# Partial sums of a graph kernel dealt out anew over its first half, and placed between two groups of count products

## Time and profile before

| | |
|---|---|
| median of three runs | 971.59 us |
| the profiled execution | 978.19 us, of which the span is 976.4 us |
| TensorE (matmul) busy | 858.0 us, 88% of the span |
| VectorE, ScalarE, GpSimd busy | 637.5, 418.0, 648.1 us |
| mean granted clock of TensorE | 0.85 of full |
| first gather to last gather | 47.3 to 722 us |
| first gate products of the second half | 765.2 us |

### The profile page before, as it was taken

One profiled execution on the slowest core, in us unless ns is written; L12 is line 12 of the kernel. 1 busy time (PEld: TensorE's weight loads), 2 busy tenths in 40 slices (PEclk: granted clock), 3 DMA queues, 4 the chain that ended last, 5 costly groups with the idle time before them and its releaser, 6 DMA issues.

```text
span 976.4 us, 15073 instructions
## 1 busy us (share of the span) xinstructions
PE 858.0 (88%) x5101; PEld 690.2 (71%) x5101; DVE 637.5 (65%) x1329; ACT 418.0 (43%) x811; POOL 648.1 (66%) x975
## 2 busy tenths in 40 slices
PE   5955797769988988999999998999988999999795
PEld 5845585556767887877788876888875666666473
DVE  5353677676776759677976785777754354556853
ACT  5522345543554546454665544555522221111241
POOL 4598988888888888888888888888860011111000
PEclk9955658785676669678999997999968999999998
DMA  9355133444444444454555554455542465555210
GB/s 201 71 124 161 55 68 96 129 124 123 99 135 99 111 116 128 130 127 121 142 153 155 147 143 111 117 150 153 139 109 64 123 189 147 156 160 177 74 37 21
DMA packets 59396, 119.20 MB, mean 122 GB/s; under 512 B 16593, under 2 KB 36751, under 8 KB 56189
## 3 DMA queue, kind: packets, MB, share of 16 engines
q1 hardware_dynamic: 39810, 93.29, 30.2%
q0 software_dynamic: 18448, 24.82, 15.7%
q10 hardware_dynamic: 1056, 0.07, 0.1%
HBM read 81.34 MB, written 36.68 MB: 121 GB/s over the span
## 4 chain that ended last, share of the span: by engine, by line
POOL 49%; PE 32%; issue 7%; DVE 7%; DMA 3%; SPq 1%; ACT 1%; DVEq 0%; ACTq 0%; POOLq 0%
POOL shared L836 25%; POOL cnt_rows L841 13%; POOL zs_third L836 11%; PE bank L2285 7%; PE bank L2315 4%; PE bank L2117 4%; PE bank L2284 3%; PE bank L2170 3%; PE bank L2037 2%; PE bank L2316 2%; DVE zus L1113 2%; DMA shared<-zu_table,src_col 1%; PE bank L2202 1%; PE bank L1940 1%; PE bank L2220 1%
## 5 line engine op out<-in xcount | busy, mean ns | idle before, releaser
L836 POOL DMA_INDIRECT shared<-zu_table,src_col x306 | 297.4, 972 | 52.1 <-issue 49.2
L841 POOL MEMSET cnt_rows<- 54x300 f32 x450 | 165.2, 367 | 0.3
L836 POOL DMA_INDIRECT zs_third<-zu_table,src_col x144 | 140.9, 978 | 23.2 <-issue 23.2
L2037 PEld LDWEIGHTS bank<-zus,shared 125*128 125x128 f32 x900 | 139.1, 247 | 16.8 <-issue 13.1
L2037 PE MATMUL bank<-zus,shared 125*128 125x64 f32 x900 | 141.4, 333 | 7.4 <-ACT setup L1803 3.0
L2170 PE MATMUL bank<-layer,oh 128*125 128x84 f32 x900 | 136.0, 325 | 0.8 <-DVE layer L1199 0.8
L2170 PEld LDWEIGHTS bank<-layer,oh 128*125 128x125 f32 x900 | 133.3, 240 | 1.1 <-issue 1.1
L1113 DVE TENSOR_TENSOR setup<-iota_b,bank 128x500 bf16<-128x500 bf16 (+1 forms) x224 | 124.5, 609 | 8.0 <-PE bank L2242 7.8
L1746 ACT ACTIVATE shared<-shared,node_id 125x2304 f32<-125x2304 int32 x25 | 55.4, 2216 | 97.5 <-PE bank L2037 59.0
L859 POOL DMA_DIRECT2D shared<-counts_table x22 | 11.7, 535 | 101.9 <-PE bank L2285 90.9
L1803 ACT ACTIVATE setup<-bank 125x500 bf16<-125x500 f32 (+1 forms) x91 | 57.3, 680 | 49.7 <-PE bank L2242 48.4
(11 more groups left out here) (254 smaller groups left out, 1700.4 us busy)
## 6 DMA issues: line engine op xcount, KB each, us to landing
shared<-in_edges SPq DMA_DIRECT2D x25, 1125.0 KB
own_table<-own_out SPq DMA_DIRECT2D x25, 375.0 KB
counts_table<-setup SPq DMA_DIRECT2D x13, 683.6 KB
shared<-own_table SPq DMA_DIRECT2D x14, 448.0 KB
counts_table<-cnt_rows SPq DMA_DIRECT2D x9, 683.6 KB
shared<-zu_table,src_col POOLq DMA_INDIRECT x306, 3.8
zs_third<-own_table SPq DMA_DIRECT2D x7, 448.0 KB
h_table<-h2s SPq DMA_DIRECT2D x25, 125.0 KB
```

Of the source, the lines that this page charges most:

```text
L836: nc.gpsimd.indirect_dma_start(out=zs[t % 3][:, j * KR:(j + 1) * KR], out_offset=None, in_=zu_table, in_offset=bass.IndirectOffsetOnAxis(a ...
L841: nc.gpsimd.memset(idle[t >= FIRST], 0.0).then_inc(idle_set, 1)
L2037: last = mm(ps(c, 128, (j - a) * KR, (j - a + 1) * KR), ohT[:, j * 128:(j + 1) * 128], zus[0:W, t, :], start=True, stop=True)
```

## The change

The begun sums are dealt out anew. Windows 13 to 20 are summed two steps later from the staging buffer, with t + 1 blocks up to 18 (14, 15, 16, 17, 18, 18, 18, 18); windows 0 to 12 are all summed from reloaded counts, in steps 9 to 21, with one block less than the step's number up to 14 (8, 9, 10, 11, 12, 13 in steps 9 to 14, then 14). There are 295 begun blocks instead of 273.

In steps 9 to 14 the 7 blocks behind `sum_rows` and the 1 to 6 behind group 4 are gone, and 8 to 13 reloaded blocks stand in one piece behind group 5. In steps 15 to 20, 14 blocks stand behind `sum_rows`, 0, 1, 2, 3, 4, 4 behind group 4, and 14 reloaded ones behind group 5; in step 21, 18 behind `sum_rows` and 14 behind group 5; in step 22, 18 behind `sum_rows`. So the reloaded blocks now stand between count groups 5 and 6, no longer ahead of group 5. In step 22, 21 products of a constant with itself (125x128 by 128x250, bf16, into an idle part of bank 2, read by nobody) stand in that place.

Sums from reloaded counts of windows 0 to 12 use the other half of bank 5, and each kind waits only for the last copy out of its own half. The copies out move: those of `keep_part` in the middle of steps 15 to 22 go, in steps 16 to 20, to the start of the next step, beside the other one. There are 13 reloads of 437.5 KB instead of 7.

```diff
-        FOLLOW = 7
+        FOLLOW = 13
+        TURNS = 7
+        LARGEST = 18
         MOST = 14
         SINGLE = 19
-        AGAIN = {15 + n: t for n, t in enumerate((1, 2, 3, 4, 5, 6, 0))}
+        AGAIN = {9 + n: t for n, t in enumerate((1, 2, 3, 4, 5, 6, 0, 7, 8, 9, 10, 11, 12))}
+        STEP_OF = {t: step for step, t in AGAIN.items()}
...
-            return t >= FOLLOW and t % 2 == 1 or t >= SINGLE
+            return t >= TURNS and t % 2 == 1 or t >= SINGLE
...
-            return 0 if t not in PARTS else min(t + 1, MOST) if t >= FOLLOW else MOST
+            return 0 if t not in PARTS else min(t + 1, LARGEST) if t >= FOLLOW else min(STEP_OF[t] - 1, MOST)
 
         def early_blocks(t):
-            return MOST if t + 2 in AGAIN or t >= SINGLE else MOST // 2
+            return LARGEST if t >= SINGLE else MOST
 
         def middle_part(t):
-            return t - 2 if t - 2 in PARTS[FOLLOW:] and early_blocks(t - 2) == MOST else None
+            return t - 2 if t - 2 in PARTS[FOLLOW:] and begun(t - 2) <= early_blocks(t - 2) else None
...
+        def part_sums(t):
+            return ps(5, W, D, 2 * D) if t < FOLLOW else ps(5, W, 0, D)
...
                 if counts:
                     count_ahead(t - 1, 3)
                     count_ahead(t - 1, 4)
-                begin_sum(t - 2, early_blocks(t - 2), MOST)
+                begin_sum(t - 2, early_blocks(t - 2), LARGEST)
+                if counts:
+                    count_ahead(t - 1, 5)
                 if t in AGAIN:
                     begin_sum_again(t)
+                if t == AHEAD:
+                    keep_clock(7)
                 if counts:
-                    count_ahead(t - 1, 5)
                     count_ahead(t - 1, 6)
+
+            def keep_clock(blocks):
+
+                for n in range(3 * blocks):
+                    mm(ps(2, W, D, D + 2 * W).rearrange("p (a w) -> p a w", a=2), iota_b[:, :],
+                       iota_b[:, :].unsqueeze(1).broadcast_to([128, 2, W]), start=True, stop=True)
...
                 pe.wait_ge(l_again, AGAIN_BASE + 32 * (step - min(AGAIN) + 1))
-                pe.wait_ge(part_kept, nth_part(t) - 1)
-                part_blocks(t, again, 0, MOST)
+                pe.wait_ge(last_third, begun(t))
+                pe.wait_ge(a_col, 3 * len(GROUPS))
+                if parts_before(t):
+                    pe.wait_ge(part_kept, parts_before(t))
+                part_blocks(t, again, 0, begun(t))
```

More of the change, by code:

```diff
@@ L264, in begun, with last_parts, parts_before @@
         def begun(t):
-            return 0 if t not in PARTS else min(t + 1, MOST) if t >= FOLLOW else MOST
+            return 0 if t not in PARTS else min(t + 1, LARGEST) if t >= FOLLOW else min(STEP_OF[t] - 1, MOST)
         def early_blocks(t):
-            return MOST if t + 2 in AGAIN or t >= SINGLE else MOST // 2
+            return LARGEST if t >= SINGLE else MOST
         def middle_part(t):
-            return t - 2 if t - 2 in PARTS[FOLLOW:] and early_blocks(t - 2) == MOST else None
-        def last_part(t):
-            return AGAIN[t] if t in AGAIN else t - 2 if t - 2 in PARTS[FOLLOW:] and middle_part(t) is None else None
-        PART_ORDER = [p for t in range(NW) for p in (middle_part(t), last_part(t)) if p is not None]
+            return t - 2 if t - 2 in PARTS[FOLLOW:] and begun(t - 2) <= early_blocks(t - 2) else None
+        def last_parts(t):
+            follows = [t - 2] if t - 2 in PARTS[FOLLOW:] and middle_part(t) is None else []
+            reloaded = [AGAIN[t]] if t in AGAIN else []
+            return follows + reloaded
+        PART_ORDER = [p for t in range(NW) for p in [middle_part(t)] + last_parts(t) if p is not None]
+        assert sorted(PART_ORDER) == list(PARTS)
         def nth_part(t):
             return PART_ORDER.index(t) + 1
+        def part_sums(t):
+            return ps(5, W, D, 2 * D) if t < FOLLOW else ps(5, W, 0, D)
+        def parts_before(t):
+            same = [p for p in PART_ORDER[:nth_part(t) - 1] if (p < FOLLOW) == (t < FOLLOW)]
+            return nth_part(same[-1]) if same else 0
         def part_out(t):
@@ L637, in prefetch @@
                     store_counts(t - 2)
-                if last_part(t - 1) is not None:
-                    store_part(last_part(t - 1))
+                for n in last_parts(t - 1):
+                    store_part(n)
                 store_own(t - 2)
@@ L1697, in attend @@
                 cuts(t + 1, 1 - h)
-                if last_part(t - 1) is not None:
-                    keep_part(last_part(t - 1))
+                for n in last_parts(t - 1):
+                    keep_part(n)
                 if t >= 2:
@@ L1726, in keep_part @@
                     act.wait_ge(st_part, 16 * (nth_part(t) - 2))
-                nc.scalar.activation(part_out(t), ps(5, W, 0, D), ACT.Copy).then_inc(part_kept, 1)
+                nc.scalar.activation(part_out(t), part_sums(t), ACT.Copy).then_inc(part_kept, 1)
             def own_transposed(t):
@@ L2101, in begin_sum @@
                     pe.wait_ge(a_col, 3 * len(GROUPS))
-                    if nth_part(t) > 1:
-                        pe.wait_ge(part_kept, nth_part(t) - 1)
+                    if parts_before(t):
+                        pe.wait_ge(part_kept, parts_before(t))
                 part_blocks(t, staged_in(t), lo, min(hi, begun(t)))
@@ L2116, in part_blocks @@
                     for m in range(3):
-                        last = mm(ps(5, W, 0, D), counts[:, a * W:(a + 1) * W], thirds(a)[:, m, :],
+                        last = mm(part_sums(t), counts[:, a * W:(a + 1) * W], thirds(a)[:, m, :],
                                   start=a == 0 and m == 0, stop=a == begun(t) - 1 and m == 2)
```

## The result

The changed kernel takes **983.55 us** (median of 8 runs, 981.02 to 985.92) against 974.39 for the kernel before (8 runs, 968.56 to 978.32): a ratio of 1.0082, 95% interval 1.0052 to 1.0111. The forecast was 1008, slower by 3.4%. The sign is right and the size is four times too large: measured by its ratio the change costs 0.8%, clear of noise and inside the band of 1% on which the prediction put 0.19. The profiled execution took 983.28 us (span 981.2, mean clock 0.862), that of before 978.19 (976.4, 0.850).

The account below looks back on a forecast made before the run. The first half was taken as a race between GpSimd's gathers (26.6 us a step) and TensorE (25.8). From 978.2, 7.2 - 5.9 - 4.2 = -2.9 and +39 for clock falls gave 1014.3, or 1008 from the median; range 962 to 1033.

Parts of the forecast that it names:

- The gaps: Waits ahead of group 5: 2.31 us in steps 9 to 15, 21, 22; 1.0 to 2.0 in 16 to 20.
- Steps 15 to 21: Uncovered wait for group 5 makes each step 28.1 us, above the gathers' 26.6; +7.2 us without clock falls.
- The clock: TensorE's clock drops to half behind gaps; falls cost 6.5 us each, +39 us in all after 6.3 of room.
- Three from 15 on, at 6.5 us: Three clock falls from step 15 on, each costing 6.5 us: 19.5 us.
- four falls in steps 9 to 14: Four clock falls in these steps at 6.5 us each, less 6.3 us of room: 19.7 us.
- Steps 9 to 14: New block order is 6.3 us quicker without falls, counted only as room to absorb clock falls.
- Step 22 and the last steps: Added blocks 1.3 and constant products 2.3 us, less 9.5 saved by holding the clock: -5.9 us.
- Rival C: Constant products in step 22 do not hold the clock; the 9.5 us come back, about 1017; no separate chance.
- The second half: 22 fewer blocks, limited by a floor of 6.18 us a step; windows 14 to 20 save 4.2 us.
- Reloads at no cost: Six more reloads of 437.5 KB on SyncE's queue delay nothing: 0 us, bound 0 to 8.
- A: Gaps ahead of group 5 open but the clock holds: 969 us, up to 982; chance 0.20.
- B: In steps 15 to 21 the wait for group 5 shrinks: 961.5 us, possibly 957; chance 0.13.

Follow-up runs that it names:

- placement-alone kernel: The kernel before with only the reloaded blocks moved between count groups 5 and 6 in steps 15 to 21; 991.16 us against 970.26, one run.
- the change without placement: The changed kernel with the reloaded blocks back ahead of count group 5 in steps 9 to 21; 973.12 us against 970.26 on chip F, one run.

## Why the prediction was right in sign and wrong in size

- **The gaps** are where predicted and, but for those of steps 13 and 14, as long: 2.31 us in steps 9 to 12 and 15 (2.62 in step 13, 1.31 in step 14, where TensorE had just waited for a gather), 1.98, 1.65, 1.36, 0.99 and 1.00 in steps 16 to 20, 2.31 in steps 21 and 22. Reading the rule off was enough.
- **Steps 15 to 21**: 28.1 us a step forecast, 28.0 measured where the clock held. +7.2 forecast without falls; +10.9 measured with falls of 6.8 and 3.4 us, which cost 5.1 and leave +5.8.
- **The clock, the step that failed.** "Three from 15 on, at 6.5 us" and "four falls in steps 9 to 14": the count was right, four early (one of them beside the waits of step 14) and three from step 15 on, step 22's included. The price was not: half of 3.4 us for five of them and half of 6.8 for two, 15.3 us in all, 2.2 a fall, where 7 x 6.5 = 45.5 stood. The 30 us between them are nearly the whole of the 31 by which the profiled execution missed the 1014.3. I had priced a fall from rows in which a few count products, dense f32 products and 36 target rows follow the gap. The text even says that what follows a gap is denser now and should end some falls earlier, and then goes only from 8.5 to 6.5. The sums behind the gap were the term to price, not the gap. That the count came right is partly luck: six of the eight gaps of 2.3 us or more brought a fall, none of the four of 1.3 to 2.0, and the seventh fall came from a place that the forecast doesn't name.
- **Steps 9 to 14**: falls of 8.5 us less 6.3 of room would be +2.2; +1.0 measured.
- **Step 22 and the last steps**: -5.9 forecast, -6.0 measured, in part by luck. The constant products took 3.81 us here, part of it at half clock, where 2.3 stood, and the target and edge rows 4.13 and 4.11, as forecast; what was saved must then be 11.1 us, where 9.5 stood, and the two misses cancel. Rival C is refuted.
- **The second half**: -4.2 forecast, -3.3 measured. The periods came as worked out, 6.49 for window 14 and then the floor, which TensorE's timeline of the kernel after shows as a wait for ScalarE's copy; it answers to the earlier trace rows:

```profile
887.31 0.32 PE L2337 MATMUL bank<-relw,cnt_rows 51*125 51x256 bf16 x1 [0.43 <-ACT layer L1847]
...
893.48 0.32 PE L2337 MATMUL bank<-relw,cnt_rows 51*125 51x256 bf16 x1 [0.43 <-ACT layer L1847]
...
913.82 0.43 PE L2330 MATMUL bank<-ident,layer 125*128 125x125 f32 x2 [3.27 <-DVE layer L1369]
```

  893.48 - 887.31 = 6.17 us, forecast 6.18. Window 20 is where it went wrong: 0.64 less was forecast, it took 11.41 instead of 10.66. With fewer blocks TensorE waits 3.27 us for VectorE's sum there (1.77 before), and the clock falls to 0.50 from 914.7 to 921.5, which it doesn't in the trace of before: a stall paid in both ways again.
- **Reloads at no cost**: the waits for gathers shrank, no new one is put down to them.
- **The rivals.** A (gaps open, the clock holds, 969 and "up to 982 with a couple of falls") had the better mechanism: dense sums do protect the clock, though they shorten falls rather than prevent them. It had 0.20 and deserved more than half; the measured 983.55 lies just above its 982. B is refuted: the wait for group 5 is 2.31 us in step 21 as in step 7. By the rule of the Trainium skill that the prediction cites ("TensorE: Matmul & The Clock Gate", "Why this matters for your kernels": gaps of under about 3 us), no gap here would cost the clock. That remains wrong (four falls behind seven gaps of 2.31 us in the placement-alone kernel, at about 1.7 us each), but its sum, 975.3 for the profiled execution, misses by 8.0 us and mine by 31.0.

## What to carry to other kernels

A stall of TensorE is paid twice, in its own length and in the clock behind it, and the second price depends on what the engine does next: read how long the half-clock stretch is behind gaps that are followed by the work that yours will be followed by. Use independent dense work as cover ahead of the late operand rather than behind it; if it cannot stand ahead, behind it still saves most of the clock (falls of 3.4 us instead of 17 and more). Where two engines run neck and neck (26.6 us of gathers, 25.8 of TensorE), anything above the difference comes out at the end, and on another chip, or on the same one at another time, the slack may not be there.

## What the hardware showed that I had not expected

A fall behind a gap of 2.3 us or more mostly lasts 17.0 to 27.3 us with f32 row products behind it (34.1 once, 3.4 in 5 of 52 falls), and 3.4, at most 6.8, with block products (bf16, 256 columns) or constant products. Which of several equal gaps brings a fall, and what made the five falls short that had nothing dense behind them, was not settled.

The same kernel before took 968.6 to 1116 us, and in the traces of its variants only the first half differs. Busy time up to the first gates of the same kernel, the change without placement, on chips F and C shows it:

```profile
0.00:761.50 761.50, 647.80 (x4178) 550.20 (x4178) 517.47 (x1097) 372.23 (x716) 626.43 (x937) 0.84 0.49 126
0.00:898.90 898.90, 726.98 (x4178) 598.66 (x4178) 522.36 (x1097) 373.77 (x716) 628.83 (x937) 0.77 0.42 107
```

From the first gates to those of window 20 both take 144.2 us. Up to them VectorE and GpSimd are busy for nearly the same time. TensorE is not: its same 4178 products take 79 us more, at a mean granted clock of 0.77 instead of 0.84, so that a part of the 137 us is the clock. GpSimd now waits for buffers. Its waits on chip C:

```profile
POOL shared L849 <- DVE layer L1212: 60.9, 9, 12.0
```

On chip F it waits only for its own issue there, 0.2 us at the longest. TensorE's waits on chip C:

```profile
PE bank L2221 <- issue: 15.2, 5, 4.9
```

These are waits of up to 4.9 us for nothing that the profile shows. What holds its instructions back there, and so what starts the loss, was not settled.
